# Attention and MLP kernel on one core: the first 30 microseconds put in another order

## The reference, cut to what matters

```python
xn = layernorm(x)                       # no scale or shift
mixed = xn @ Wqkv.T                     # 768 columns: q, k, v of 16 heads of 16
attn = softmax((q @ k.T) / 4)           # per batch and head, 256 x 256
s = (attn @ v) @ Wproj.T + bproj
h = gelu(xn @ proj1.T + proj1_bias)     # 256 -> 1024
g = silu(h @ proj2.T + proj2_bias)      # 1024 -> 256
out = x + s * g
```

## Time and profile before

| | us |
|---|---|
| three timed runs | 144.46, 146.15 (median), 147.87 |
| the profiled execution | 144.28 |
| its span | 142.5 |
| TensorE busy | 128.7 (90%) |
| TensorE weight loads busy | 98.2 (69%) |
| VectorE busy | 84.0 (59%) |
| ScalarE busy | 77.0 (54%) |
| GpSimd busy | 51.5 (36%) |

### The profile page before, as it was taken

The page is one execution under the profiler, slowest core; times in us unless marked ns, Lnnn a source line. Parts: engine busy times, 40 slices in busy tenths (PEclk is TensorE's granted clock), DMA queues, the critical chain, the costliest instruction groups (busy, mean ns, idle before and its releaser), DMA issues.

```text
span 142.5 us, 2709 instructions
## 1 busy us (share of the span) xinstructions
PE 128.7 (90%) x1028; PEld 98.2 (69%) x1028; DVE 84.0 (59%) x170; ACT 77.0 (54%) x115; POOL 51.5 (36%) x53
## 2 busy tenths in 40 slices
PE   6679979999999899989899879999999999999760
PEld 5359868988897888766566556676776677777440
DVE  0658855200007999999999943264465346435942
ACT  3063358979960110043564797976667856875210
POOL 3178106999980000005536430693013004000620
PEclk9999999999999999999999999999999999999997
DMA  4799589999999998000000070000011001101102
GB/s 131 215 431 408 155 163 147 151 145 152 163 154 173 168 169 123 21 5 2 0 9 5 14 285 14 9 5 0 0 41 37 0 5 37 37 2 41 39 0 74
DMA packets 7440, 13.28 MB, mean 93 GB/s; under 512 B 900, under 2 KB 2564, under 8 KB 7172
## 3 DMA queue, kind: packets, MB, share of 16 engines
q1 hardware_dynamic: 6996, 12.85, 41.7%
q10 hardware_dynamic: 432, 0.27, 1.0%
HBM read 5.51 MB, written 1.05 MB: 46 GB/s over the span
## 4 chain that ended last, share of the span: by engine, by line
PE 59%; DVE 27%; DMA 5%; issue 4%; ACT 2%; SPq 1%; DVEq 0%
PE bank L563 37%; DVE negm L483 21%; PE bank L680 10%; PE bank L651 8%; DMA wqkv_raw<-wqkv 5%; PE bank L689 2%; DVE gate L451 1%; PE bank L696 1%; DVE yh L524 1%; DVE fin L542 1%; ACT xTh L353 1%; PE bank L631 1%; SPq L241 1%; ACT wqh L343 0%; ACT stage L360 0%
## 5 line engine op out<-in xcount | busy, mean ns | idle before, releaser
L483 DVE TENSOR_REDUCE negm<-bank 128x4 f32<-128x1024 f32 x32 | 37.1, 1222 | 17.2 <-PE bank L631 17.2
L406 ACT ACTIVATE PT<-bank 128x1024 f32<-128x1024 f32 x32 | 31.1, 1022 | 6.8 <-PE bank L651 6.3
L318 POOL TENSOR_TENSOR hTl<-hG,hTh 128x512 fp32r<-128x512 f32 x16 | 20.4, 1308 | 30.9 <-ACT hTh L392 30.9
L328 POOL TENSOR_TENSOR bg<-gate,bps 128x256 f32<-128x256 f32 x8 | 6.1, 757 | 31.8 <-DVE gate L451 31.8
L680 PE MATMUL bank<-PT,VA 128*17 128x256 f32 x256 | 16.9, 382 | 0.0
L563 PE MATMUL bank<-w2h,hTh 128*128 128x256 f32 x64 | 15.2, 319 | 0.7 <-DVE yh L524 0.7
L388 ACT ACTIVATE hG<-bank,b1s 128x512 f32<-128x512 f32 x16 | 11.0, 688 | 8.8 <-PE bank L563 8.8
L563 PEld LDWEIGHTS bank<-w2h,hTh 128*128 128x128 f32 x64 | 9.7, 189 | 8.1 <-issue 7.2
L495 DVE COPY cd<-bank 128x256 f32<-128x256 f32 x16 | 6.8, 425 | 14.4 <-PE bank L680 14.4
L416 ACT ACTIVATE th<-yh 128x256 f32<-128x256 f32 x8 | 3.3, 418 | 21.0 <-DVE yh L524 21.0
L651 PE MATMUL bank<-qs,ks 50*128 50x256 f32 x128 | 12.3, 307 | 1.7 <-DVE negm L483 1.7
(11 more groups left out here) (75 smaller groups left out, 215.4 us busy)
## 6 DMA issues: line engine op xcount, KB each, us to landing
qs<-stage SPq DMA_DIRECT2D x12, 256.0 KB, 12.4
ks<-stage SPq DMA_DIRECT2D x12, 256.0 KB, 18.7
w_raw<-w SPq DMA_DIRECT2D x2, 1024.0 KB, 9.4
xs<-x SPq DMA_DIRECT2D x4, 256.0 KB, 6.0
xb<-x SPq DMA_DIRECT2D x1, 1024.0 KB, 5.4
out<-fin SPq DMA_DIRECT2D x8, 128.0 KB, 1.7
wqkv_raw<-wqkv SPq DMA_DIRECT2D x3, 256.0 KB, 6.9
wps<-wp SPq DMA_DIRECT2D x1, 256.0 KB, 10.6
```

Source lines behind the costliest of these rows:

```text
L318: nc.gpsimd.tensor_tensor(hTl[:, n % FC, :], hG[:, n % FC, :], hTh[:, n % FC, :].bitcast(f32), ALU.subtract).then_inc(h_lo, 1)
L328: nc.gpsimd.tensor_tensor(bg[:, u % 2, :], gate[:, u, :], bps[:], ALU.mult).then_inc(bg_done, 1)
L406: nc.scalar.activation(PT[:, w % 4], scores_of(*s), ACT.Exp).then_inc(exp_done, 1)
L483: nc.vector.tensor_reduce(negm[:, j, :, :, s[1] % 2, b].rearrange("p q a -> p a q"), scores_of(*s), axis=AX.X, op=ALU.max, negate=True).th ...
```

## The change

The loads: SyncE issues x blocks 0 to 3, then w1, the three biases, w2, wps. ScalarE issues the three chunks of Wqkv.

The order: after XT 0 comes one small product of zeros (`KEEP`), then four new entries `QA` i, which project block 0 alone (256 columns) for all four chunks, with XT 1 between the second and the third; `QK` 0, i then projects the other 256 columns of half 0 and signals. The two `V` of half 0 stand behind XT 2 and XT 3, before `QK` 1. Each `QA` i writes the same bank as its `QK`, banks 4 to 7, and the ring of projections has four banks instead of three up to the first score.

VectorE and GpSimd: the statistics are split in two (`norm_stats`, `norm_eps`), block 0 is normalised before block 1's mean is formed, and the later blocks come in turn between the low halves; GpSimd makes the root of block 1 behind the first weight chunk. The warm-up has six products instead of five, and its zeros lie elsewhere in memory.

```diff
-WARM = 5
+WARM = 6
...
-    order = [("XT", 0), ("XT", 1)] + [("QK", 0, i) for i in range(4)]
-    order += [("XT", 2), ("XT", 3)] + [("QK", 1, i) for i in range(4)]
-    order += [("V", 0, p) for p in range(2)]
+    order = [("XT", 0), ("KEEP",), ("QA", 0), ("QA", 1), ("XT", 1), ("QA", 2), ("QA", 3)]
+    order += [("QK", 0, i) for i in range(4)]
+    order += [("XT", 2), ("V", 0, 0), ("XT", 3), ("V", 0, 1)] + [("QK", 1, i) for i in range(4)]
...
+                if kind == "QA":
+                    home[s] = (4 + s[1],)
                     continue
...
-                    home[s] = (5 + turn % 3,) if n < first_s else (6 + turn % 2,)
+                    home[s] = (4 + turn % 4,) if n < first_s else (6 + turn % 2,)
...
-            for b in range(2):
-                sp.dma_start(xs[:, 2 * b:2 * b + 2, :], x_t[:, b, :]).then_inc(x_in[b], 16)
-            for c in range(3):
-                sp.dma_start(wqkv_raw[:, c], wqkv[c]).then_inc(wqkv_in[c], 16)
-            for b in range(2, B):
+            for b in range(B):
                 sp.dma_start(xs[:, 2 * b:2 * b + 2, :], x_t[:, b, :]).then_inc(x_in[b], 16)
             sp.dma_start(w1_raw[:], w1).then_inc(w1_in, 16)
+            sp.dma_start(b1s[:], b1).then_inc(bias_in, 16)
+            sp.dma_start(b2s[:], b2.to_broadcast([P, E])).then_inc(bias_in, 16)
+            sp.dma_start(bps[:], bp.to_broadcast([P, E])).then_inc(bias_in, 16)
...
             rsqrt(0)
-            rsqrt(1)
             for c in range(3):
                 pool.wait_ge(wqkv_hi, c + 1)
                 nc.gpsimd.tensor_tensor(wql[:, c], wqkv_raw[:, c], wqh[:, c].bitcast(f32),
                                         ALU.subtract).then_inc(wqkv_lo, 1)
+                if c == 0:
+                    rsqrt(1)
...
-            act.dma_start(b1s[:], b1).then_inc(bias_in, 16)
-            act.dma_start(b2s[:], b2.to_broadcast([P, E])).then_inc(bias_in, 16)
-            act.dma_start(bps[:], bp.to_broadcast([P, E])).then_inc(bias_in, 16)
+            for c in range(3):
+                act.dma_start(wqkv_raw[:, c], wqkv[c]).then_inc(wqkv_in[c], 16)
...
+                    if b == 0:
+                        norm_apply(1)
+                        norm_stats(2)
+                        norm_eps(2)
                     if b == 1:
-                        norm_stats(2)
                         norm_stats(3)
+                        norm_eps(3)
+                        norm_apply(2)
...
-                    if n_qk <= 2:
-                        norm_apply(n_qk + 1)
+                    if n_qk == 1:
+                        norm_apply(3)
...
+                elif s[0] == "KEEP":
+                    nc.tensor.matmul(bank[:, 7, 0:P], warm[:, 0:P], warm[:, 0:P], start=True, stop=True)
+                elif s[0] == "QA":
+                    pe.wait_ge(wqkv_hi, s[1] // 2 + 1)
+                    project(("QK", 0, s[1]), 0, SQ)
...
+                    last = project(s, h * HALF + (SQ if h == 0 else 0), SQ if h == 0 else HALF)
```

More of the change, by code:

```diff
@@ L139, in layer_kernel @@
         ones = at("ones", [2, SQ], f32)
-        warm = at("warm", [P, HALF // 2], f32, stage_at)
+        warm = at("warm", [P, HALF // 2], f32, stage_at + 28 * KB)
         cd = at("cd", [P, 2, SQ], f32)
@@ L195, in banks @@
                 kind = s[0]
-                if kind == "GATE" or (kind == "F2" and s[2] > 0) or (kind == "PJ" and s[2] > 0):
+                if kind in ("GATE", "KEEP") or (kind == "F2" and s[2] > 0) or (kind == "PJ" and s[2] > 0):
+                    continue
+                if kind == "QA":
+                    home[s] = (4 + s[1],)
                     continue
@@ L432, in norm_stats, with norm_eps @@
                     nc.vector.bn_stats(stats[:, t, :], xs[:, t, :]).then_inc(stats_done, 1)
+            def norm_eps(b):
                 for t in (2 * b, 2 * b + 1):
@@ L455, in _ @@
             norm_stats(0)
+            norm_eps(0)
             norm_stats(1)
             norm_apply(0)
-            norm_apply(1)
+            norm_eps(1)
             n_qk = n_mt = 0
@@ L574, in warm_up, with project @@
                     nc.tensor.matmul(bank[:, 7, 0:HALF // 2], warm[:, 0:P], warm[:], start=True, stop=True)
+            def project(s, at, width):
+                i = s[2]
+                cols = slice(at, at + width)
+                seen = KC * (cols.stop // SQ - 1)
+                return product(bank_of(*s)[:, at % HALF:at % HALF + width],
+                               lambda kc, a: (wqh, wql)[a][:, i // 2, kc, (i % 2) * P:(i % 2 + 1) * P],
+                               lambda kc, a: (xTh, xTl)[a][:, kc, cols], range(KC),
+                               rhs_hi=(xt_hi, seen), lhs_lo=(wqkv_lo, i // 2 + 1), rhs_lo=(xt_lo, seen))
             pe.wait_ge(warm_set, 1)
@@ L592, in _ @@
                     wait_free(s)
-                    cuts = [(0, SQ), (1, SQ)] if (h, i) == (0, 0) else [(h, HALF)]
-                    for n, width in cuts:
-                        cols = slice(n * width, (n + 1) * width)
-                        seen = KC * (cols.stop // SQ - 1)
-                        last = product(bank_of(*s)[:, n * width % HALF:n * width % HALF + width],
-                                       lambda kc, a: (wqh, wql)[a][:, i // 2, kc, (i % 2) * P:(i % 2 + 1) * P],
-                                       lambda kc, a: (xTh, xTl)[a][:, kc, cols], range(KC),
-                                       rhs_hi=(xt_hi, seen), lhs_lo=(wqkv_lo, i // 2 + 1), rhs_lo=(xt_lo, seen))
+                    last = project(s, h * HALF + (SQ if h == 0 else 0), SQ if h == 0 else HALF)
                     last.then_inc(qk_made, 1)
```

## The result

| | before | after |
|---|---|---|
| median of the timed runs (four each) | 145.32 us | 147.78 us |
| lowest and highest | 144.46, 147.87 | 147.54, 148.35 |
| profiled execution | 144.28 | 147.54 |
| its span | 142.5 | 145.7 |
| start of the first score product, S(0) | 43.04 | 42.91 |

The ratio is 1.0191, with a 95% interval from 1.014 to 1.0241: the changed kernel is slower. The forecast was 1.1 us faster. A ratio compares only the executions of each kernel within 1.5% of its fastest, so it can differ from the ratio of the medians, which are of all runs. The last two lines of the table say where to look. At S(0) the changed kernel is 0.13 us ahead, at the start of the transposed scores 0.52 behind, at the end 3.26 behind.

The account below looks back on a forecast made before the run. Bound by the second weight chunk's transfer to 9.09 us, mostly TensorE to 43, then VectorE's maxima. The first `w1l` product comes 1.1 us earlier: 144.28 - 1.1 = 143.2 profiled, 146.15 - 1.1 = 145.0 median; range 142.8 to 147.8.

Parts of the forecast that it names:

- Transfers: Loads at the start: second weight chunk and x1 land at 5.8 us; the weights gain over 3 us, x1 nothing.
- Head: Up to the first projection: block 0 normalised from 6.55, first projection at 8.4 instead of 10.13, 1.7 us earlier.
- Clock at the start: Rival: TensorE's clock rises late, at 14.1, during first projections; 0.9 us slower, median 147.0; chance 0.27 together with late weights.
- Projections and T: First-half projections, V and transposes take 10.2 us; T, the start of the second half's projections, comes at 18.9.
- The wait for `w1l`: Before the first MLP product with `w1l`: TensorE waits 2.0 us for GpSimd, finished at T + 8.1.
- Behind that point nothing is reordered: From the score stage at 43 us on: the gain at S(0), 1.1 us, carries through one for one.
- The stage copies: Twelve restacking DMAs of q and k ahead of S(0): gate stays at 41 to 42, gain not much above 1.2 us.
- takes away a spread as well: Rival: the longer warm-up fixes when the clock rises, removing the spread between runs; median 143.0; chance 0.16.

Follow-up runs that it names:

- loads_only: The kernel before with only the new order of the loads; 145.42 us, ratio 1.0027.
- Run 7: Also pool_apart: w1_bank_fill with GpSimd's `wql` of chunks 0 and 1 held back until blocks 0 and 1 are normalised; 142.87 us, ratio 0.9813.
- fill_after: Also run 1: the changed kernel with identity products filling TensorE's waits at the first two transposed score products; 146.63 us, ratio 1.004.
- w1_bank_fill: Also run 4: fill_after with the first F2 result in bank 6 and w1 rounded one projection earlier; 141.94 us, ratio 0.9809.
- v_only: The changed kernel with V of half 0 put back behind the second half's projections, nothing else; 145.78 us, ratio 1.0.
- v_back: fill_after with the first F2 result in bank 6 and V of half 0 back behind the second half's projections; 143.47 us, ratio 0.9894.
- fill_before: The kernel before with identity products filling TensorE's waits at the first two transposed score products; 144.13 us, ratio 0.9947.
- run 9: Also fill_both: fill_after plus nine identity products filling TensorE's wait for `w1l` ahead of the first F1; 144.95 us, ratio 1.0015.
- run 4: The same run as w1_bank_fill: fill_after with the first F2 result in bank 6 and w1 rounded one projection earlier; 141.94 us, ratio 0.9809.
- 12: pool_apart plus seven identity products filling the wait for the stage copies ahead of S(0); 143.36 us, ratio 0.9876.
- run 11: Also w1_only: the changed kernel with only the rounding of w1 one projection earlier on ScalarE; 145.13 us, ratio 0.9985.

## Why the prediction was wrong

Its forecast for a profiled execution was 143.2; it was 147.54. By the table the 4.3 us are 1.0 at S(0) (42.91 for 41.9), 0.7 for the bank, and 2.7 for the clock, give or take 0.1. The median missed by less (147.78 for 145.0) because I had added 1.9 us for the distance of the median from the profiled execution, and here that distance is 0.2: the profiled run had drawn a long stretch at half clock like the others of its comparison.

*Transfers: right.* 5.8 was worked out for the second chunk and x1; 5.6 and 5.4 came. That the biases make the dip was only my reading; now the dip has moved with them, from 4 us to 9.5, in loads_only as well. No run leaves the biases out, so it is well supported rather than shown.

*Head: 0.4 too early.* First projection 8.81 for 8.4. The term that was mis-sized is the normalisation, 1.67 us for 0.73; it began 0.46 before my 6.55, which gives half of that back. I had moved it and the early `wql` on top of each other and costed each by its row alone. Run 7 confirms it: held apart, 8.03. The Trainium skill ("SBUF — State Buffer", section "Who interferes with whom") says that VectorE and GpSimd share a pair of ports, that a tensor_scalar in a two-port mode needs them, and that whoever issues first holds them for its whole instruction. The trace agrees in kind: GpSimd's `wql` keeps its 1.27 us and the normalisation, begun 0.08 later, pays 0.94 more.

*Clock at the start: the rival fell.* Starts of 256-column products are 0.12 apart from 9.2 on, through three sets of interposed transposes. The rule of the Trainium skill that the forecast weighed (transposes don't count) didn't bring a late clock in this profile. The rival's figure, 147.0, came near the result, but its mechanism isn't what happened. In other executions it does happen: of eleven profiles with the changed head three had half the clock there, fill_after to 11.1 us, w1_bank_fill to 12.8 and v_only to some 14.3. In v_only it moved S(0) by 1.6 us (43.70 for the 42.10 of v_back); in fill_after the `w1l` product came only 0.12 later (28.07 for 27.95), as the prediction had it for a rise before 11.8. That this profile was spared was in part luck. In the old head (fill_before, a rise 0.5 us later than the 14.1 of before) S(0) came 0.3 later, 43.31 for 43.04.

*Projections and T: 19.95 for 18.9.* 8.81, 10.2 of work as worked out, and 0.80 us of waiting for the second normalisation (its row is the one at 11.62) give 19.8. The same collision once more.

*The wait for `w1l`: right.* 1.91 us for 2.0, released by GpSimd, at T + 8.0 for T + 8.1. It was the step I held to most, and I priced it wrongly all the same: as time that the chain sets anyway and so as nothing on top. Runs 1 and 9 show what an idle TensorE costs besides.

*"Behind that point nothing is reordered, so I count what the change does to the start of the first score product, S(0), and let the rest follow one for one."* This is the step that failed, and it carries 3.4 of the 4.3 us: the profiled kernel before took 101.24 us from S(0) to the end, the changed one 104.63. Two things pass through it. The ring of four banks is a change of placement; it isn't in the order of instructions, and my reading of the order couldn't show it, though the `home` line stood in the diff. And TensorE's clock can fall behind S(0), at waits that the change didn't touch: in the changed kernel it did, from 85.2 to 92.0. The timeline of the kernel before had both waits of the transposed scores (1.18 and 0.53 us), and its three runs a spread of 3.4 us. I offered a clock that rises late as the reason of that spread and didn't look for places where it might fall.

*The stage copies: right for the change, not fixed.* I put the gate at 41 to 42. The first copy was issued at 15.71 and the twelfth landed at 39.5, so S(0) at 42.91 didn't wait. In runs 4, 7 and 12 it did, until 42.35, 41.83 and 42.25; in run 11 S(0) went at 40.66 unhindered. The twelfth copy landed anywhere between 39.5 (the changed kernel) and 42.9 (v_only, which came late), and at 39.5 and 41.8 in two executions of the changed kernel itself. So the landing isn't set by the program alone, and a gate that stays at 41 to 42 was the wrong picture.

*The median of before.* The rival "takes away a spread as well" was wrong in its sign. The spread of the kernel before is there in all comparisons (4 of 29, the one of 203.42 left aside, 7 of 23 and 4 of 29 runs above 147 us), filling its waits gave a ratio of 0.9947, and the change made the bad case the usual one: none of its 16 runs is under 146.06.

The Trainium skill ("TensorE: Matmul & The Clock Gate", section "A second HAM failure mode: psum-queue depth-cycling") describes a kernel in which short waits between groups of matmuls, each small, make the clock go back and forth. The transposed scores start in such a place: 1.18 and 0.54 us within 2.2 us. The traces agree in part: with these waits and the one ahead of `w1l` filled the clock held in the profile of run 9, but where it fell here it fell once and came back, and didn't go back and forth.

What stays open. Why the changed kernel loses the clock in all 16 runs (so I read their times, all 1.2 us or more above the 42.91 + 101.94 = 144.85 of a clock that holds with S(0) as profiled, and their mean clocks, 0.946 to 0.986) and the kernel before only in some, although the waits at 82 us are alike: a dependence on what lies before, or on where in time the waits fall, is argued and not shown. The 0.52 us shift alone doesn't decide it, since v_only, at 83.68, and w1_only, at 80.65, lost the clock too, and v_only kept it (by its mean clock of 0.99) in three other runs. Nor does the fall keep a fixed distance: it came 1.4 us (w1_only) to 3.1 us (loads_only) behind the start of the first transposed score. The runs of w1_bank_fill near 141.9 were not profiled; by the table's 101.1 their S(0) was at 40.8, with no wait for the copies, which is an inference. And fill_both stands at 1.0015 while fill_before stands at 0.9947: with the clock steadied in both, the change still costs some 0.7%, about 1 us, with intervals of 0.3 and 0.4% on the two ratios. The bank is 0.7 of it and S(0) would give 0.1 back; the rest is within the intervals.

The version to keep is w1_bank_fill: the changed head, the first F2 result in a bank that no score uses, w1 rounded one projection earlier, and the waits at the transposed scores filled. 141.94 us, 1.9% under the kernel before.

## What to carry to other kernels

When work is moved ahead of a stage, look at what it used to cover where it lay: here 24 products of V hid the chain to `w1l`, and an idle TensorE cost its own time and, besides, in many executions, speed afterwards. Read a ring or a pool's new size as a move of every buffer behind it, and check who shares a bank with whom at the first place where the stages meet. To separate head from tail over many variants, subtract the start of one landmark from the total: if that difference isn't constant, something else than the order has changed.

## What the runs showed of the hardware that I had not expected

- Idle times of TensorE of 1.18 and 0.54 us, little apart, or one of 1.91 us, were followed in many executions by 3.4 or 6.8 us at the lower of its two clock levels, and in others by none. A long one costs 2.7 us of the 144; with the gaps filled by products of `ident` the profile of run 9 didn't show it and its twelve runs stayed within 1 us, at no cost in time (S(0) unchanged at 42.91).
- A pair of fp32 normalisations on VectorE (each 128 x 256, two per-partition scalars) took 0.73 us alone and 1.67, 2.20 and 2.62 beside GpSimd's subtraction of 128 x 512 elements; GpSimd's time stayed at 1.27 to 1.29 for each subtraction (1.26 apart, in pool_apart).
- While the two replicated bias rows (128 KB each) are open, there is a stretch of 1 to 1.5 us in which all 16 DMA engines together move little: 78 to 80 GB/s in the kernel before, 105 to 131 in the changed one, 58 and 63 in loads_only, against some 400 around it in the last two.
- The restacking copies of one and the same program landed 2.3 us apart in two executions (the twelfth at 39.5 and at 41.8).
